# A transformer block on one core: the first attention slots' loads and the first slot's maxima inside the projection

## What is computed

```python
x = x + attention(layernorm(x), Wq, bq, Wk, bk, Wv, bv, Wo, bo)   # causal, 32 heads
x = x + ffn(layernorm(x), gate, up, down)      # 4 bit weights: (w - zero) * scale, 128 rows a group
x = x + topk_mlp(layernorm(x), w_gate, w_up, w_down)
x = x + ffn(layernorm(x), gate, up, down)      # the same 4 bit weights
...
scores = jnp.einsum('bhqd,bhkd->bhqk', q, k) / math.sqrt(hd)
scores = jnp.where(causal, scores, -jnp.inf)
att = jax.nn.softmax(scores, axis=-1)
out = jnp.einsum('bhqk,bhkd->bhqd', att, v)
```

## Time and profile before

| | |
|---|---|
| runs | 2035.01, 2042.77, 2043.76 us, median 2042.77 |
| profiled execution, own time | 2038.18 us |
| its span | 2036.4 us |
| PE busy | 1875.8 us, 92% |
| projection, last matmul ends | 153.8 us after the span's start |
| first slot's maxima on DVE | 166.6 to 187.7 us |
| first shifted score | 194.1 us |
| last division of the attention on DVE ends | 641.5 us |

### The profile page before, as it was taken

One profiled execution on the slowest core, in us unless ns is written; L12 is line 12 of the kernel. 1 busy time (PEld: TensorE's weight loads), 2 busy tenths in 40 slices (PEclk: granted clock), 3 DMA queues, 4 the chain that ended last, 5 costly groups with the idle time before them and its releaser, 6 DMA issues. The chain is left out here.

```text
span 2036.4 us, 40240 instructions
## 1 busy us (share of the span) xinstructions
PE 1875.8 (92%) x15312; PEld 1164.8 (57%) x15312; DVE 1483.7 (73%) x2424; ACT 1043.4 (51%) x1981; POOL 624.5 (31%) x791
## 2 busy tenths in 40 slices
PE   7995898999896798999999999999999999999989
PEld 3442333333332475775766667676776766757756
DVE  6545887888881412998889889797898898888941
ACT  4331777777775122663554545545635636546411
POOL 3693554655662410111103112121121121211221
PEclk9995999999998999999999999999999999999999
DMA  7764445545433712003130130113121031031000
GB/s 239 227 193 115 114 107 128 137 129 140 140 110 103 237 61 91 22 1 112 57 112 1 57 108 26 56 68 122 47 87 57 1 122 34 24 122 57 12 11 11
DMA packets 127037, 183.16 MB, mean 90 GB/s; under 512 B 46232, under 2 KB 83096, under 8 KB 126896
## 3 DMA queue, kind: packets, MB, share of 16 engines
q1 hardware_dynamic: 119808, 163.12, 26.1%
q0 software_dynamic: 4064, 12.65, 2.0%
q10 hardware_dynamic: 3024, 5.51, 0.7%
HBM read 147.39 MB, written 33.62 MB: 89 GB/s over the span
## 5 line engine op out<-in xcount | busy, mean ns | idle before, releaser
L1311 POOL TENSOR_TENSOR lohi<-h,lohi 128x256 f16<-128x256 f32 x224 | 174.0, 777 | 872.0 <-ACT lohi L1463 871.8
L1452 ACT ACTIVATE kept<-ax,T 128x1376 f16<-128x1376 f32 x248 | 357.3, 1441 | 121.6 <-DVE T L1526 115.7
L1520 DVE TENSOR_SCALAR_CACHE_REDUCE junk<-ax,T 128x1376 f16<-128x1376 f32 x248 | 406.5, 1639 | 2.7
L884 DVE TENSOR_REDUCE mx<-s 128x2 f32<-128x1024 f32 (+2 forms) x320 | 341.1, 1114 | 78.4 <-PE s L761 40.9
L860 ACT ACTIVATE pr<-s 128x512 f32<-128x512 f32 (+2 forms) x640 | 320.3, 553 | 124.9 <-PE s L789 105.8
L1349 PE MATMUL ga<-xT_f,w_gate 128*128 128x256 f16 x2688 | 332.8, 274 | 7.6 <-DVE h L1577 4.6
L1359 PE MATMUL acc<-w_down,lohi 128*128 128x512 f16 x1344 | 326.2, 379 | 8.8 <-POOL lohi L1311 8.7
L1349 PE MATMUL ub<-xT_f,w_up 128*128 128x256 f16 x2688 | 331.6, 273 | 0.0
L1349 PEld LDWEIGHTS ga<-xT_f,w_gate 128*128 128x128 f16 x2688 | 263.4, 98 | 79.7 <-DVE h L1577 7.2
L1349 PEld LDWEIGHTS ub<-xT_f,w_up 128*128 128x128 f16 x2688 | 263.9, 98 | 31.2
L1577 DVE SCALAR_TENSOR_TENSOR h<-ub,g 128x256 f32<-128x256 f32 x224 | 94.2, 420 | 165.6 <-ACT g L1458 164.3
(11 more groups left out here) (152 smaller groups left out, 2643.4 us busy)
## 6 DMA issues: line engine op xcount, KB each, us to landing
ring<-wgu_scr SPq DMA_DIRECT2D x64, 688.0 KB, 5.3
ring<-wd_scr SPq DMA_DIRECT2D x24, 768.0 KB, 4.7
wgu_scr<-tk_h POOLq DMA_DIRECT2D x32, 172.0 KB, 2.7
q_scr<-qk_h SPq DMA_DIRECT2D x16, 256.0 KB, 2.7
k_scr<-qk_h SPq DMA_DIRECT2D x16, 256.0 KB, 4.6
v_scr<-v_f SPq DMA_DIRECT2D x16, 256.0 KB, 4.7
Q<-q_scr SPq DMA_DIRECT2D x64, 64.0 KB, 2.1
K<-k_scr SPq DMA_DIRECT2D x64, 64.0 KB, 2.1
```

The source lines that it names most:

```text
L884: nc.vector.tensor_reduce(dst.rearrange("p (t j) -> p t j", t=NT)[:, :, p0:p1], scores.rearrange("p t (j k) -> p t j k", k=w), AX.X, ALU.m ...
L1311: nc.gpsimd.tensor_tensor(hT[j % 2][:, 1, :], h[j % 2][:, :], hT[j % 2][:, 0, :], ALU.subtract).then_inc(hl_ok, 1)
L1452: nc.scalar.activation(kept[0][:, :], ax[k % 2][:, 1, :], ACT.Sign, scale=-1.0, bias=TF[:, 1:2], accum_out=cnt[:, 1:2]).then_inc(c1_ok, 1)
L1520: nc.vector.tensor_scalar(junk[:, :], ax[k % 2][:, 0, :], TF[:, 0:1], -float(KZERO), ALU.is_lt, ALU.add, accum_out=cnt[:, 0:1]).then_inc(c ...
```

## The change

- A class `Scores` holds what both blocks use: Q and K buffers, `V0`, maxima, masks, semaphores. It is allocated ahead of the projection. To make room, the projection's raw q, k, v weights lie in the memory of `w_down`, whose pieces are dequantised in the attention.
- POOL makes the masks, identities and row of ones right after the second reciprocal root of chunk 0; SP spreads them at turn 11 (8 DMAs).
- SP loads Q and K within the projection: slot 0 after turns 15 and 25, slot 1 after turns 28 and 30 (8 DMAs each), V of slot 0 after turn 32. The stores that these loads read are waited for on SP.
- The projection's turns 34 to 47 also hold the 20 maxima units of slot 0 and the transpose: two in one turn, then one, and so on. They use `a_tr` banks, which are free then. The row from `mxT` is issued by SP after its last v store, ahead of its wait for all stores.
- The attention block starts at once with slot 0: its first items are maxima units of slot 1, whose Q and K are there. SP's first items are V of slot 1 and the 13 loads of weight pieces.

```diff
-        w_raw = sb("w_raw", [P, 3, KB, D], F32)
+        w_raw = spare[:, 0:2 * 3 * KB * D].bitcast(F32).rearrange("p (m k n) -> p m k n", m=3, k=KB)
...
+        FIRST_AT = SLOTS - SPC - 2
+        first_units = {s: [] for s in range(SLOTS)}
+        for k in range(N1 + 1):
+            first_units[FIRST_AT + k * (SLOTS - FIRST_AT) // (N1 + 1)].append(k)
+        first_rows = {SPC + 3: (0, 0), 2 * SPC + 1: (0, 1), 2 * SPC + 4: (1, 0), 2 * SPC + 6: (1, 1)}
...
+                if s == SPC - 1:
+                    sc.spread_constants(sp)
+                if s in first_rows:
+                    n, f = first_rows[s]
+                    sp.wait_ge(qk_st[0], 16 * QK_SLOTS // NST * (f + 1))
+                    sc.load_qk(sp, n, f)
+                if s == 2 * SPC + QK_SLOTS:
+                    for i in range(NSV):
+                        sp.wait_ge(v_st[i], 16 * TPC // NSV * (NCH // B))
+                    sc.load_v(sp, 0, sc.V0)
+            sc.maxima_row(sp, 0)
...
             root(1, 0, 2)
             root(2, 2, TPC)
+            sc.constants(pool)
...
+                for k in first_units[s]:
+                    if k < N1:
+                        sc.maxima(dve, tr2, 0, k)
+                    else:
+                        sc.maxima_join(dve, 0)
+                        sc.maxima_end(dve, tr2, 0)
...
+                for k in first_units[s]:
+                    if k == 0:
+                        pe.wait_ge(xl_ok, TPC * NCH)
+                        pe.wait_ge(sc.cst2, 64)
+                    if k < N1:
+                        sc.maxima_unit(pe, tr2, 0, 0, 0, k)
+                    else:
+                        sc.maxima_transpose(pe, tr2, ident, 0)
...
-            for n in range(2):
-                for f in range(2):
-                    load_qk(n, f)
...
-                load_v(n)
+            load_v(1)
             load_pieces(0)
-            maxima_row(0)
...
-            pe.wait_ge(cst2, 64)
-            pe.wait_ge(one_in[0], 32)
...
-            for u in range(N1):
-                maxima_unit(0, 0, 0, u)
-            maxima_transpose(0)
-            pe.wait_ge(one_in[1], 32)
             slot(0, 0, 0, first=True)
...
-            for u in range(N1):
-                maxima(0, 0, 0, u)
-            maxima_end(0, 0, 0)
```

More of the change, by code:

```diff
@@ L115, in build @@
                          *(keep.enter_context(nc.semaphore(f"dq_{n}")) for n in ("sub", "up", "mul", "hi", "lo")))
-        phase_project(nc, x, WqT, bq, WkT, bk, WvT, bv, pieces, FIRST_PIECES, dq, ident, q_scr, k_scr, v_scr)
-        phase_attend(nc, ident, q_scr, k_scr, v_scr, o_scr, pieces, FIRST_PIECES, dq, wgT, wuT, wdT, wgu_scr, wd_scr)
+        with ExitStack() as near:
+            sc = Scores(nc, near, q_scr, k_scr, v_scr)
+            phase_project(nc, x, WqT, bq, WkT, bk, WvT, bv, pieces, FIRST_PIECES, dq, ident, sc,
+                          w_down[:, :, :, :].rearrange("p a j n -> p (a j n)"), q_scr, k_scr, v_scr)
+            phase_attend(nc, ident, sc, o_scr, pieces, FIRST_PIECES, dq, wgT, wuT, wdT, wgu_scr, wd_scr)
         phase_output(nc, x, WoT, bo, ident, o_scr, x1_scr)
@@ L168, in phase_project @@
         dq_f = dq_w[:, :, :].bitcast(F32)
-        ptr = [pb(f"a_tr{i}", [P, KB, P], F32) for i in range(NTR)]
+        tr2 = [pb(f"a_tr{i}", [P, NTR // 2 * BANK], F32) for i in range(2)]
+        ptr = [tr2[i // 2][:, i % 2 * BANK:(i % 2 + 1) * BANK].rearrange("p (k t) -> p k t", k=KB) for i in range(NTR)]
         pmm = [pb(f"a_mm{i}", [P, CW], F32) for i in range(4)]
@@ L247, in _ @@
                     load_piece(dq_load[s])
+                if s == SPC - 1:
[9 more added lines that the diff above has]
+            sc.maxima_row(sp, 0)
             for i in range(NST):
                 sp.wait_ge(qk_st[i], 16 * QK_SLOTS // NST * NCH)
-                sp.wait_ge(v_st[i], 16 * TPC // NST * NCH)
+            for i in range(NSV):
+                sp.wait_ge(v_st[i], 16 * TPC // NSV * NCH)
         @block.gpsimd
@@ L454, in _, with maxima_units @@
                     transposes(c + 1, t)
[L457 to L478, removed]
+                for k in first_units[s]:
[6 more added lines that the diff above has]
+                        sc.maxima_transpose(pe, tr2, ident, 0)
+QH = 4
+NQ = B * H // QH
+GPB = H // QH
+QR = QH * HD
+NB = L // P
+NT = 2
+NP = QH // NT
+RT = P // NT
+KR = 3 * HD
+BANK = 512
+HALF = NB // 2
+QK_DMAS = 16 * 4 * NT
+def maxima_units():
+    units = []
     for qb in range(NB):
@@ L486, in phase_attend @@
+def phase_attend(nc, ident, sc, o_scr, pieces, done, dq, wgT, wuT, wdT, wgu_scr, wd_scr):
     groups = [(f, kb, max(kb * P - f * BANK, 0)) for f in range(2) for kb in range((f + 1) * BANK // P)]
```

269 lines of the change are left out of this document (145 added, 124 removed).

## The result

| | before | changed |
|---|---|---|
| median of the runs on one chip | 2038.89 us (2034.22 to 2043.76, 4 runs) | 2014.82 us (2013.63 to 2018.73, 4 runs) |
| ratio, 95% interval | | 0.9892 (0.9867 to 0.9917) |
| profiled execution, its span | 2038.18, 2036.4 | 2015.89, 2014.1 |

What follows compares the result with a forecast made beforehand. Bound: PE's pace, with a 40.3 us serial handover before slot 0. Replacing it by P 9 and H 6.0 gains 25.3 us: 2012.9 from the profile, 2017.5 from the median; predicted 2015, range 2004 to 2029.

Steps and rivals of the forecast that it cites:

- The bound: Projection to slot 0: barrier, loads, DVE's reductions and one small DMA form a 40.3 us path; starting earlier moves the rest.
- P: Cost of the 20 units inside the projection: 5.6 columns, 1.9 DVE waits, 2.0 group changes; 9 us taken, 5.6 to 14.
- 14 and 8 us: High ends of the units' cost in the projection and of the handover, said to leave a gain of 18.5 us.
- the dearer sum: Units' cost in the projection if every DVE subtraction were as long as the longest, 1.48 us: 11 to 12 us.
- H: Handover, last projection matmul to first shifted score: bias, transpose, DMA landing, barrier, three units; 6.0 us, between 5.5 and 8.
- Slot 0, nothing: First attention slot: counted as slow as before, its first 10.2 us at clock 0.50, so 0 us won.
- warm handover: Rival, 0.13: clock stays up or returns at once at the handover, slot 0 saves some 4 us; about 2010.
- The clock within the turns: Projection's last turns, sign of being right: PE's clock stays 1.00 until the barrier.
- the clock falls inside the projection's last turns: Rival, 0.05: PE's stops between turns drop its clock to 0.50; first shifted score 19 us later, 2059.
- Edits at nothing: POOL's masks, 41 more SP DMAs at 0.47 us each, `w_down`'s place, V beside ones: all expected to cost nothing.
- Everything from the output phase on moved by the same amount: Sign of being right: phases behind the attention come earlier by one equal amount.
- The last projection matmul: End of the projection on PE, sign of being right: at 161 to 165 us.

Runs made afterwards that it cites:

- e2: Changed kernel with the projection's maxima reductions reading only 16 columns of a tile instead of up to 512; 2011.02 us, one time.
- e3: Changed kernel with the same 20 units and transpose in the projection's last 8 turns instead of 14; 2031.67 us, 0.9968 of before.
- e9: Changed kernel with the same 20 units in the projection's last 10 turns instead of 14; 2025.34 us, one time.
- e6: Changed kernel with twelve extra matmuls, result unread, on PE behind the transpose of the first slot's maxima; 2015.87 us, 0.9900 of before.
- e8: Changed kernel with POOL issuing the constants' DMAs, twelve unread matmuls behind the maxima's transpose, first Q and K loads at turn 23; 2009.74 us, 0.9854 of before.
- e4: Changed kernel with the eight DMAs that spread the constants issued by POOL instead of SP at turn 11; 2012.47 us, 0.9876 of before.
- e10: The kernel before, unchanged, profiled a second time; 2028.67 us, one time.

## Why the prediction was right, and where not

**The bound.** Right: barrier, loads, serial reductions and one small DMA were the path, and what started the first shifted score earlier moved the rest. 23.5 us earlier there became 22.3 in the span of the two profiles (447 to 445 in the attention, 3.2 given back in the rest) and 24.1 in the medians.

**P, the units within the projection, 9.** The turns grew by 9.5, the count before it was rounded. Its parts: PE's columns and changes of group were put at 7.6 and measured 8.1, DVE's waits at 1.9 and measured 1.4 (e2). The count turn by turn gave DVE its right role, and e3 and e9 show how near its edge 14 turns are. The prediction's sums hold, with one slip: 14 and 8 us give a gain of 18.3 at the low end, not 18.5, which moves nothing. The twelve large reductions took 1213 ns in the turns, with POOL busy for 28.8 of 43.2 us, and 1219 in the serial block of before, with POOL busy for 3.7 of 23.0. In the later slots the median is the same, the second figure here:

```profile
L649 DVE TENSOR_REDUCE mx<-s x300: 681/1215/1228, 169.4 to 584.7; 128x2 f32<-128x1024 f32 x90, 128x4 f32<-128x512 f32 x30, 128x2 f32<-128x768 f32 x30
```

The subtractions took 0.95 us in the mean, less than the 1.03 of the earlier trace rows and not 1.48, so that P was not 11 to 12. Laid beside POOL's rows, the 17 subtractions in the profiles of before and of the changed kernel during which POOL was idle took 0.67 to 0.69 us, and every one of 0.73 us or more, up to 1.62, ran beside a dequantising step of POOL. So the trace agrees with both halves of what the Trainium skill (SBUF — State Buffer, "Who interferes with whom") states, that a VectorE instruction with two SBUF inputs contends with GpSimd reading SBUF and a `tensor_reduce` never does; only the dearer sum did not come, since one of the eight subtractions in these turns reached 1.48 us, and the others took 0.67 to 1.25.

**H, 6.0.** 5.57 from the last matmul to the first shifted score. `mxT` stood at 1.5 rather than 1.9, the barrier at 3.4 in place of 3.8, and three units of slot 1 came first, as in the order. The row from `mxT` was not waited for.

**Slot 0, nothing.** Right: 27.5 us at 0.81, as before. The warm handover did not come by itself; e6 and e8 show that it was there to be had, for 2.3 to 3.1 us.

**The clock within the turns.** Right for this kernel: 1.00, with no wait for the maxima above 0.52 us inside the turns. The mechanism of the rival "the clock falls inside the projection's last turns" is real all the same: e3 and e9, made after the prediction, show it behind waits of 2.70 and 1.94 us, once each and at a price of 1.1 and 1.4 us.

**Edits at nothing.** The step that failed, by 2.0 us. The text had "Eight in a row take 3.7 us", of which "PE's four banks cover" ACT's 1 us. They took 5.7 us on SP, 0.7 each and not 0.47. The 0.47 is the distance between loads of Q and K; the trace of before already had these very DMAs, eight of them in 5.3 us. SP's queue there, one row of 0.60 left out:

```profile
160.72 1.43 SPq L604 DMA_DIRECT2D K<-onerow  x2
162.19 1.18 SPq L644 DMA_DIRECT2D identx<-identb  x2
...
164.04 0.60 SPq L646 DMA_DIRECT2D mask_k<-mask_k  x1
...
172.96 1.29 SPq L604 DMA_DIRECT2D K<-onerow  x2
```

ACT did stand 0.9 us, but the cover was looked for in the wrong place: not PE's banks but DVE's normalisation, queued behind the late subtractions, and PE's transposes behind that. The text's own price for a lost cover, "1 to 3 us", was right. For the loads of Q and K, POOL's masks and `w_down`'s place nothing was right (e4: 74.48 against 74.51, with all of them in place).

**Everything from the output phase on moved by the same amount.** Wrong by 3 us, which e10 places at the clock; what in the change brings it is open.

**The last projection matmul** at 165.05 is at the edge of the 161 to 165 that the text gave; 2.3 us of its distance to 162.8 are the two misses above (2.0 before turn 34 and 0.5 by rounding, 0.2 less in the first loads). That the median came within 0.2 us of the forecast is partly luck: 2015 was a middle between 2012.9 and 2017.5, for two values of before, and before itself had a median of 2038.89 in the comparison and not 2042.77. The sum against the profiled execution was 2012.9, and its counterpart took 2015.9: 2.3 us lost before the handover, 0.4 won in it, 2.0 won in the attention by the clock's chance, 3.2 lost in the rest.

## What to carry to other kernels

Work that waits for a barrier in series (loads, then matmuls with a reduction each) can be taken into the phase ahead, and costs there its own work on the engine that sets the pace (5.6 us of columns here, 8.1 with the changes) and what the helping engine has too little room for: count that engine turn by turn and spread the work. With DVE counted at 80% of PE's time (14 turns) PE's waits cost 1.4 us; crowding the same units into 8 turns gave nearly half of the gain back. Count every DMA that is put into a busy issuing queue at its own length there, ask what stands behind it, and give it to an engine that is idle at that time (2 us here). Compare profiles by distances between common rows, since two profiles of one kernel differed by 6.9 us in the attention, mostly by the clock.

## What the runs showed of the hardware

- A pause of PE of 0.9 and 2.4 us around one transpose, behind 43 us of work at clock 1.00, was followed by more than 10 us at 0.50; twelve matmuls in the pause kept 1.00 (e6, e8).
- Waits of PE between turns, of 2.57 and 2.70 us some 4 us apart (e3) and one of 1.94 (e9), were followed by a turn at clock 0.50, 3.82 and 4.12 us instead of 2.76; waits of up to 0.52 us in the changed kernel's turns were not.
- A subtraction of 128x512 on DVE took 0.67 to 0.69 us with POOL idle and up to 1.62 beside POOL's dequantising; reductions took 1213 ns beside it and 1219 with POOL mostly idle.
- DMAs that copy from SBUF to SBUF took SP 0.6 us each to issue, once 1.30 (`mask_k`), where the loads of Q and K at turn 15 took 0.41 to 0.45; POOL issued the same eight in 4.3 us, 0.5 each.
- The same code of the output and MLP phases ran some 3 us longer behind a changed earlier phase, in eight profiles of eight against two, with PE's clock coming back later.
- The same kernel took 2028.67 to 2046.21 us over these runs; of the 9.5 us between its two profiles 6.9 lie in slots with a fallen clock.
